# Attention and quantised feed-forward on one core: the steps of the attention loop issued in pairs around their projection pieces, with a third tile bank, one norm bound per batch and a new opening

## The reference, cut to what matters

```python
x = x + attention(layernorm(x), ctx, ctx, mask, Wq, Wk, Wv, Wo)
x = x + ffn(layernorm(x), rhs)

def attention(Q, K, V, mask, Wq, Wk, Wv, Wo):          # heads of 32
    q, k, v = Q @ Wq.T, K @ Wk.T, V @ Wv.T             # split into 16 heads
    e = exp(clip(q @ k^T / sqrt(32), -50, 50))         # 1024 x 2048 per head and batch
    out = where(mask, e / sum(e), 0) @ v
    return out @ Wo.T

def ffn(lhs, rhs):                                      # int8, one scale per row / column
    ql, qr = round(lhs / row_scale), round(rhs / col_scale)
    return (ql @ qr) * row_scale * col_scale
```

## Time and profile before

| what | us |
|---|---|
| median of 3 runs (lowest, highest) | 1937.39 (1935.2, 1943.0) |
| the profiled execution: its time / its span | 1937.39 / 1935.6 |
| TensorE (PE) busy | 1815.8, 94% |
| VectorE (DVE) busy | 1533.6, 79% |
| ScalarE (ACT) busy | 1296.8, 67% |
| GpSimd (POOL) busy | 284.2, 15% |
| DMA, mean | 143 GB/s |

### The profile page before, as it was taken

One profiled execution on the slowest core, in us unless ns is written; L12 is line 12 of the kernel. 1 busy time (PEld: TensorE's weight loads), 2 busy tenths in 40 slices (PEclk: granted clock), 3 DMA queues, 4 the chain that ended last, 5 costly groups with the idle time before them and its releaser, 6 DMA issues.

```text
span 1935.6 us, 31331 instructions
## 1 busy us (share of the span) xinstructions
PE 1815.8 (94%) x10584; PEld 995.7 (51%) x10584; DVE 1533.6 (79%) x1857; ACT 1296.8 (67%) x1682; POOL 284.2 (15%) x200
## 2 busy tenths in 40 slices
PE   5887999999998999999999999999999999999986
PEld 4775555555554555655555565555556333333333
DVE  4335789888886989888898988889898788878875
ACT  3334777777776676776767677677767676767752
POOL 0000011111110212111111211112121112111123
PEclk9998999999998999999999999999999999999997
DMA  6458264645556364665736456473645544546232
GB/s 217 142 177 229 78 158 126 172 121 149 142 153 160 103 171 117 159 165 147 187 102 172 121 144 178 136 192 101 178 116 134 151 128 102 153 103 154 61 115 98
DMA packets 224933, 276.36 MB, mean 143 GB/s; under 512 B 27520, under 2 KB 142208, under 8 KB 224128
## 3 DMA queue, kind: packets, MB, share of 16 engines
q1 hardware_dynamic: 224768, 274.28, 52.7%
HBM read 181.41 MB, written 92.54 MB: 142 GB/s over the span
## 4 chain that ended last, share of the span: by engine, by line
PE 63%; issue 11%; DVE 10%; DMA 8%; ACT 4%; SPq 3%; POOL 2%; DVEq 0%; POOLq 0%; ACTq 0%
PE tile L705 21%; PE scores L743 19%; PE wsum L757 17%; DVE acc L1142 5%; ACT probs L918 2%; DMA den_c<-denoms 2%; PE dsum L769 1%; DMA v_parts<-v_stage 1%; DMA row_lo<-o_parts 1%; DMA denoms<-recip_row 1%; SPq L528 1%; PE tile L837 1%; POOL normed L1199 1%; DMA k_parts<-stage_hi 1%; SPq L540 1%
## 5 line engine op out<-in xcount | busy, mean ns | idle before, releaser
L918 ACT ACTIVATE probs<-scores 128x1024 f32<-128x1024 f32 x1024 | 993.6, 1024 | 377.8 <-PE scores L743 375.0
L1142 DVE TENSOR_TENSOR acc<-acc,probs 128x1024 f32<-128x1024 f32 x864 | 1085.0, 1294 | 87.1 <-ACT probs L918 85.4
L743 PE MATMUL scores<-q_stack,k_stack 128*128 128x512 f32 x2048 | 634.9, 429 | 8.6 <-ACT probs L918 6.3
L743 PEld LDWEIGHTS scores<-q_stack,k_stack 128*128 128x128 f32 x2048 | 339.9, 190 | 512.0 <-ACT probs L918 333.9
L757 PE MATMUL wsum<-probs,v_sb 128*32 128x512 f32 x4096 | 549.5, 608 | 0.5
L1186 POOL TENSOR_TENSOR rstd<-var_eps,minus_half 128x1 f32<-128x1 f32 x56 | 53.2, 951 | 834.4 <-DVE var_eps L1044 834.4
L757 PEld LDWEIGHTS wsum<-probs,v_sb 128*32 128x32 f32 x4096 | 81.7, 108 | 152.7 <-issue 74.5
L1142 DVE TENSOR_TENSOR acc<-probs 128x1024 f32<-128x1024 f32 x64 | 76.5, 1221 | 99.5 <-PE dsum L769 97.8
L705 PE MATMUL tile<-ctx_hi,wk_hi 128*128 128x256 f32 x448 | 127.8, 285 | 21.0 <-DVE wk_lo L998 17.9
L705 PE MATMUL tile<-ctx_hi,wk_lo 128*128 128x256 f32 x448 | 126.9, 283 | 0.0
L705 PE MATMUL tile<-ctx_lo,wk_hi 128*128 128x256 f32 x448 | 126.3, 282 | 0.0
(11 more groups left out here) (153 smaller groups left out, 1807.9 us busy)
## 6 DMA issues: line engine op xcount, KB each, us to landing
k_stack<-k_parts SPq DMA_DIRECT2D x256, 256.0 KB, 5.8
q_stack<-q_parts SPq DMA_DIRECT2D x128, 256.0 KB, 7.1
v_parts<-v_stage SPq DMA_DIRECT2D x64, 256.0 KB, 3.2
v_sb<-v_parts SPq DMA_DIRECT2D x64, 256.0 KB, 5.2
raw<-ctxT SPq DMA_DIRECT2D x28, 512.0 KB, 5.8
k_parts<-stage_hi SPq DMA_DIRECT2D x96, 128.0 KB, 3.3
k_parts<-stage_lo SPq DMA_DIRECT2D x96, 128.0 KB, 3.3
k_parts<-q_stack SPq DMA_DIRECT2D x64, 128.0 KB, 3.7
```

The costliest lines, as they stand in the source:

```text
L743: last = nc.tensor.matmul(scores[:, h, :], k_stack[:, kt // 4, h, (kt % 4) * P:(kt % 4 + 1) * P], q_stack[:, qb, h, :], start=True, stop=True)
L918: nc.scalar.activation(probs[:, slot % RING, 2 * pair:2 * pair + 2, :], scores[:, 2 * pair:2 * pair + 2, :], ACT.Exp, scale=1.0 / math.sqr ...
L1142: nc.vector.tensor_tensor(acc[:, heads, :], other, now, ALU.add).then_inc(sems["add_done"], 1)
```

## The change: what it does

- **Pairs.** TensorE does, per two slots: the scores of the even slot, the pieces of both slots, the scores of the odd slot, then the sums of the two slots before. ScalarE: the even exponentials, the copies out of the pieces, the odd exponentials, the rest. VectorE: the even add, the early work (K, Q, X, N, O, F) of both slots, the odd add, the late work (`split`, `stats`, `apply`, `quant`). An add is now one instruction of 128x2048.
- **Third tile bank.** `dsum` becomes the third bank of `tile`; V and O of segments with stage A use it when no denominators are under way. In the opening 7 banks are used in turn.
- **Norm bound.** Each K and Q tile's squares are folded into a running maximum (two or three small maxima on VectorE), and N is one piece per batch (8 matmuls of 128 columns) in place of 3 per segment (4 of 256 columns each).
- **Order.** A new `BOTH`; stage C's rows are loaded within the segment (`orows`), the result is stored by an event `out` of its own. The denominators are made before the last two sums of a half.
- **Opening.** The preparation of the other weights and of `rhs` lies within the four opening segments; the first x rows are normalised and transposed at the start.
- The normalisation on GpSimd becomes multiply, copy, subtract (it was multiply, multiply, subtract).

```diff
@@ two rows of the table BOTH, and the pair loop on TensorE @@
-    18: [("K", 1, 2), ("X", 1)], 19: [("load_x", 2), ("K", 1, 3)],
+    24: [("K", 1, 3)], 25: [("V", 1, 0, 0), ("apply", 1), ("whole", 1)],
+    26: [("T", 1), ("X", 1)], 27: [("V", 1, 0, 1), ("V", 1, 0, 2)],
...
-                for slot in range(STEPS):
-
-                    summing = seg.prev and slot < LAG or seg.b and slot >= LAG
-                    for pair in range(2):
-                        if seg.b:
-                            scores_of(slot, pair)
...
-                    if summing:
-                        for pair in range(2):
-                            sums_of(slot - LAG, pair)
+                for even in range(0, STEPS, 2):
+                    if seg.b:
+                        scores_of(even)
+                    for slot in (even, even + 1):
+                        for p in seg.pieces(slot):
+                            piece(slot, p)
+                    if seg.b:
+                        scores_of(even + 1)
+                    if seg.prev if even == 0 else seg.b:
+                        if (even - 2) % KT == KT - 2:
+                            denoms_of(even - 2)
+                        sums_of(even - 2)
+                        sums_of(even - 1)
@@ scores_of: its waits are as before @@
+                    for pair in range(2):
+                        ct.wait(pe, "exp_done", 2 * n + pair - 1)
...
@@ banks @@
+            if not seg.b:
+                bank = ring % 7
+                ring += 1
+            elif seg.a and key[0] in "VO":
+                bank = D_BANK
+            else:
+                bank = 4 + turn % 2
+                turn += 1
@@ ScalarE @@
+                for even in range(0, STEPS, 2):
                     if seg.b:
+                        exponentials(even)
+                        for slot in (even, even + 1):
+                            for p in seg.pieces(slot):
+                                evacuate(p)
+                        exponentials(even + 1)
+                        for slot in (even, even + 1):
+                            for p in seg.at(slot):
+                                work(p)
@@ VectorE @@
-                                other = probs[:, (slot - 1) % RING, heads, :] if first else acc[:, heads, :]
-                                nc.vector.tensor_tensor(acc[:, heads, :], other, now, ALU.add).then_inc(sems["add_done"], 1)
+                    other = probs[:, (slot - 1) % RING, :, :] if first else acc[:, :, :]
+                    nc.vector.tensor_tensor(acc[:, :, :], other, probs[:, slot % RING, :, :], ALU.add).then_inc(sems["add_done"], 1)
...
+                for even in range(0, STEPS, 2):
+                    if seg.b:
+                        add(even)
+                        for soon in (True, False):
+                            for slot in (even, even + 1):
+                                for p in seg.at(slot):
+                                    if (p[0] in SOON) == soon:
+                                        row_work(p)
+                            if soon:
+                                add(even + 1)
@@ norm bound: the squares of K and Q on VectorE, N on TensorE @@
+                        nc.vector.tensor_tensor(run if opens else both[:, 0:P], both[:, 0:P], both[:, P:2 * P], ALU.max) \
+                            .then_inc(sems["maxed" if opens else "folded"], 1)
...
+                        if not opens:
+                            folded += 1
+                            ct.wait(dve, "folded", folded)
+                            nc.vector.tensor_tensor(run, run, both[:, 0:P], ALU.max).then_inc(sems["maxed"], 1)
...
-                            sq += KC
-                            ct.wait(pe, "squared", sq)
+                        ct.wait(pe, "maxed", seg.count("K", "Q"))
@@ GpSimd @@
-                nc.gpsimd.tensor_tensor(o_hi[:, :], sums[:, :], denoms[:, :], ALU.mult).then_inc(sems["attn_normed"], 1)
                 nc.gpsimd.tensor_tensor(sums[:, :], sums[:, :], denoms[:, :], ALU.mult).then_inc(sems["attn_normed"], 1)
+                ct.wait(pool, "attn_normed", 2 * k - 1)
+                nc.gpsimd.tensor_copy(o_hi, sums[:, :]).then_inc(sems["attn_normed"], 1)
```

More of the change, by code:

```diff
@@ new lines, with alone, add @@
+    30: [("out", 1), ("V", 1, 1, 1)], 31: [("V", 1, 1, 2), ("split", 2), ("flag",)],
+}
+def alone(n):
+    plan = {
[5 rows of a table added]
+    }
+    def add(slot, *events):
+        plan[slot] = list(events) + plan[slot]
+    if n == 0:
+        add(0, ("stats", -2), ("apply", -2), ("stats", -1), ("apply", -1))
+        add(1, ("weight", 1))
+        add(2, ("weight", 2))
+        add(4, ("X", -2), ("X", -1))
+        add(5, ("load_x", 0), ("load_x", 1))
+    else:
+        plan[0][2:2] = [("load_x", 0), ("load_x", 1)]
+    if n == 1:
+        add(2, ("prep", 0))
+        add(4, ("prep", 1))
+        add(6, ("weight", 3))
+    if n == 2:
+        add(1, ("R",))
+        for c in range(KC):
+            add(2 + c, ("prep", 2 + c))
+    if n == 3:
+        for c in range(KC):
+            add(1 + c, ("U", c))
+    return {slot: [q for p in events for q in ([p + (third,) for third in range(THIRDS)] if p[0] == "V" else [p])] for slot, events in plan.items()}
@@ L90, with __init__ @@
+PIECES = "KVXQOTFNRU"
+SOON = "KQXNOF"
+STAGE_C = ("O", "T", "F", "orows", "tail_rows", "load_xr", "quant", "whole", "out")
+AHEAD = (("X", 0), ("X", 1), ("stats", 0), ("stats", 1), ("apply", 0), ("apply", 1), ("load_x", 0), ("load_x", 1), ("load_raw", 2), ("split", 2))
+PER_BATCH = ("N", "bound", "flag")
 DIRECT = (3, 8)
+D_BANK = 6
 class Segment:
-    def __init__(self, a, b, c, prev, more, batches, parts, direct=(), last_a=False):
-        self.a, self.b, self.c = a, b, c
+    def __init__(self, s, a, b, c, prev, batch, part, direct=()):
+        self.s, self.a, self.b, self.c = s, a, b, c
@@ L98, in __init__ @@
         self.prev = prev
-        self.last_a = last_a
-        self.more = more
-        self.batches, self.parts = batches, parts
-        self.n = (batches[1] - batches[0]) * (parts[1] - parts[0])
-        self.plan = BOTH if b else ALONE
+        self.batch, self.part = batch, part
+        self.last_a = a and batch == B - 2 and part == G - 1
+        self.last_b = b and batch == B - 1 and part == G - 1
+        plan = BOTH if b else alone(s) if a else {}
+        self.plan = {slot: [p for p in events if self.keeps(p)] for slot, events in plan.items()}
@@ L607, in iteration @@
                         load_v(j, 3)
-                    if seg.b and seg.more:
+                    if seg.b and not seg.last_b:
                         if slot == 17:
@@ L765, in sums_of @@
                     last.then_inc(sems["step_summed"], 1)
-                    if kt == KT - 1:
-                        ct.wait(pe, "add_done", 2 * seg.adds * (2 * (n // STEPS) + qb + 1))
-                        for h in range(G):
-                            last = nc.tensor.matmul(dsum[DH * h:DH * h + DH, :], ones[:, :], acc[:, h, :],
-                                                    start=not (seg.direct_before if n < 0 else seg.direct), stop=True)
-                        last.then_inc(sems["acc_summed"], 1)
@@ new lines, in denoms_of @@
+                def denoms_of(n):
+                    half = 2 * (n // STEPS) + n % STEPS // KT
+                    direct = seg.direct if n >= 0 else seg.direct_before
+                    ct.wait(pe, "add_done", seg.adds * (half + 1))
+                    if not direct:
+                        freed(last_d[0])
+                    for h in range(G):
+                        last = nc.tensor.matmul(dsum[DH * h:DH * h + DH, :], ones[:, :], acc[:, h, :], start=not direct, stop=True)
+                    last.then_inc(sems["acc_summed"], 1)
@@ L976, in _ @@
+            runs(body, between)
             last_rows_scalar(act)
```

833 lines of the change are left out of this document (415 added, 418 removed), and 32 rows, old and new, of tables (ALONE, BOTH, plan).

## The result

The changed kernel takes 2000.12 us (median of 4 runs, 1987.13 to 2003.51) where the kernel before takes 1937.16 beside it (1935.2 to 1943.0): ratio 1.0302, 95% interval 1.0259 to 1.0346. It is slower by 3%, where 1882 us, faster by 3%, was forecast (range 1828 to 1928). The profiled execution, the longest of the four, took 2003.51 us, its span is 2001.7, the mean granted clock of TensorE 0.941 (before 0.982). The clock has two levels, 0.50 (1.2 GHz) and 1.00, so twice what is missing to 1 is the share of time at the low one: 2 x 0.059 x 2001.7 = 236 us, where it was 2 x 0.018 x 1935.6 = 70.

What follows compares the result with a forecast made beforehand. TensorE's list and what holds it up were taken as the bound. Opening 150, A+B 397.5, A+B+C 885.9, last batch 377.2 and end 69.5 make 1880.1; with 1.8 around it 1882 us against 1937.4, range 1828 to 1928.

Steps and rivals of the forecast that it cites:

- What bounds the kernel: From the second stage on, TensorE's list sets the length (busy 883 of 911 us); other engines matter where they delay it.
- Pairs: Steady stages: a pair takes the larger of 5.3 us and 3.95 plus its pieces, where 4.28 stood.
- X: A+B+C, second transpose of x: TensorE waits 7.3 us for VectorE and GpSimd (bounds 1.2 and 10); A+B 3.8.
- Other waits stay covered: A+B+C segments: the remaining waits stay hidden, VectorE working about 98 of 112 us, as before.
- the 1.1 foreseen: Middle of an A+B+C segment: smaller waits, 0.8 us at T and 0.3 at the denominators.
- The clock behind a wait: A+B+C: 1.2 GHz for 3.4 us adds 1.7 us to each wait of 7 us, none to those of 3.8.
- Last batch: Pairing costs: 90.7 us a segment against 89.2, plus waits of 2.7 (denominators) and 0.9; 377.2 us in all.
- Opening: First stage: 150 us for 182.2 (bounds 145 and 170), 7 banks letting TensorE run ahead of ScalarE and VectorE.
- the end: Last stage: keeps 69.5 us, its chain through GpSimd having the same three operations.
- Rival 3: Last batch: the clock falls in bare pairs, at TensorE pauses of 0.8 and 0.4 us; 2000 us; chance 0.08.
- Rivals 1 and 4: First, chance 0.14: X hardly waits, 1817 us; other, 0.08: VectorE bounds A+B+C, 117 a segment, about 1922 us.
- Rival 2: A+B and A+B+C: mode changes stay, 4.15 us per pair, 1920 us; or opening held by stores, 1912; chance 0.20.

Runs made afterwards that it cites:

- experiment 5: Changed kernel with X (1) at slot 29, second-half K tiles one slot or more later, key and query loads at slots 5 and 9: 1841.72 us.
- Experiments 2 and 3: Changed kernel, one edit each: second-half K tiles one slot or more later, 63 us saved; key and query loads moved to slots 5 and 9, 53 us saved.
- Experiment 4: Changed kernel plus 24 unused matmuls before X (1) and 12 before K (1, 0): median 20 us lower, 113 us less at half clock.
- experiment 6: The kernel of experiment 5 with TensorE and ScalarE going slot by slot again in the last batch alone: 1820.54 us.

## Why the prediction was wrong, point by point

**What bounds the kernel: right.** TensorE's list and what holds it up decided every run.

**Pairs: right in A+B and A+B+C.** K with a third takes 3.39 + 2.87 = 6.26 us (predicted 6.3; before 6.61), a bare pair 5.27 (5.3). With the three waits gone (experiment 5) the whole of A+B came out within 1 us.

**X: right in place and cause, its price partly by luck.** Wait and clock together cost 9.2 us (7.3 + 1.7 predicted), but as 6.7 of wait in the mean and 2.5 of clock. A+B's slot 26 took 6.57 against 2.90 with X at 29, 3.7 for 3.8, of which only 2.5 were the wait; there no clock had been counted.

**The step that failed: "Other waits stay covered".** Two were not, and they make the miss. In A+B+C, slots 3 and 4 took 6.07 + 5.24 for 2.87 + 3.38: 5.1 us. Slots 16 and 17 took 13.09, for 3.95 + K 1.41 + T 0.25 + denominators 0.89 + the 1.1 foreseen = 7.6: 5.5 us. Together 10.6 a segment, and (856.5 - 782.6) / 7 is 10.6 too. A+B has the same two: slots 3 and 4 3.8 over, 16 and 17 (10.56 for 6.25) 4.3, which makes 32 us in four segments for a miss of 28.8. I had gone through VectorE's total (98 of 112 us) in place of its order at the place where K(1, 0) needs `split`, and had not followed, on SyncE's queue, the stores of the Q tiles to their new place behind the loads of slot 0. Experiments 2 and 3 remove each alone; with X they turn 3% slower into 5% faster.

**The clock behind a wait: too small.** I allowed 1.7 us behind X's wait and nothing behind others, from a spell of 3.4 us at 0.50. Here spells of 3.4, 6.8 and 10.2 us go with waits of 3.42, 3.92 and 6.48 us. TensorE works for 2.92 + 5.75 + 5.95 = 14.6 us of these 20.4, so up to 7.3 us a segment are lost by the clock. Experiment 4 measures 2.1 us of it behind K(1, 0) and 2.5 behind X. For X itself the low guess did not show, since its wait was 0.6 shorter than counted.

**Last batch: direction right, size off by 10 us.** Slots 16 and 17 took 11.12 us (slot 17 alone 8.24), where 5.3 + 0.89 + the two waits, 2.7 and 0.9, make 9.8. The waits were smaller than that (0.84 to 0.87 us for T, 1.0 to 1.4 for the denominators); what was not counted is again the clock. The first of the four segments, T and denominators, and the window behind:

```profile
1598.58 0.38 PE L892 MATMUL tile<-ident_bf,q 128*128 128x128 bf16 x4 [0.84 <-ACT q L994]
...
1602.45 1.94 PE L838 MATMUL tile<-acc,ones 128*32 128x512 f32 x8 [1.41 <-DVE acc L1230]
1601.20:1608.00 6.80, 5.55 (x25) 1.26 (x26) 3.49 (x2) 2.09 (x4) 0.00 (x0) 0.50 0.01 1
```

Slots 26 and 27 took 1.2 more than 5.3 + 0.89, slots 0 and 1 0.9 more.

**Opening: right.** 154.8 for 150, within its bounds; **the end** gained 3.6 where none was expected.

**Rival 3, the clock falling in bare pairs: wrong in its mechanism**, though its time of 2000 us was met, by luck. With pauses of 0.64 and 0.18 us in every pair the granted clock stayed 1.00 over the 40 us shown in experiment 6. Where it fell, longer waits stood: those of 2.1 to 7.7 us in A+B and A+B+C, and at slots 16 and 17 of each of the last batch's four segments those of 0.84 to 0.87 and 1.0 to 1.4 us, with pauses of 0.44 and 0.18 between them. The rule of the Trainium skill, "TensorE: Matmul & The Clock Gate", section "A second HAM failure mode: psum-queue depth-cycling", that short idles between groups can make the clock alternate, is not borne out for the bare pairs' pauses; for those of slots 16 and 17 the trace agrees, with 6.8 us at 0.50 each time.

**Rivals 1 and 4** fell: X waited, and VectorE's total was not the bound in A+B+C. **Rival 2** fell with the pair lengths.

## What to carry to other kernels

When instructions are regrouped, list for every piece the one instruction that it needs and what now stands ahead of that in its own queue, DMA queues too: totals of busy time hide a producer that became one add late. A wait that names ScalarE may be a store behind loads. And a wait of a few microseconds on TensorE can cost more than its length, because the half clock reaches behind it (2.1 us behind a wait of 3.9, 2.5 behind one of 6.7): where two places are equal, put the piece where it surely does not wait, but look one consumer further (X at 30 made the queries wait).

## What the runs showed of the hardware

GpSimd is slowed by VectorE's long two-input adds more than by short ones. In the kernel before, beside adds of 128x1024, the power of 128x1 took 951 ns in the mean; beside 128x2048 it took 2178 in the changed kernel; in the opening, before there are such adds, one took 548. Each starts with an add and ends just after it (922.62 + 2.57 for the add at 922.49 + 2.29). A cast of 128x512 took 2.55 us in the same segment. Halved adds lower the mean to 1338. VectorE's add stretches as well, to 3.35 us. The Trainium skill, "GPSIMD Engine Reference", section "1. Specifications", says that GpSimd's SBUF interfaces are shared with VectorE, with contention for instructions with two SBUF inputs; the trace agrees, and here the length of VectorE's instruction counts.
